# Recurrent stage of a fused attention and mixture kernel: decay spread two units ahead, gather two units behind, three buffers

## The reference, cut to what matters

```
q, k, v = x @ Wq, x @ Wk, x @ Wv                     # x normalised; 16 heads of 8
gk = log_sigmoid(x @ Wg1 @ Wg2 + bg2) / 16
S_t = exp(gk_t)[..., None] * S_{t-1} + k_t[..., None] * v_t[..., None, :]   # 8x8 state per head
o_t = einsum('bhdv,bhd->bhv', S_t, q_t) * 8**-0.5
o = o * rsqrt(mean(o * o) + 1e-5) * g_norm_w
out = (o * silu(x @ Wg)) @ Wo
```

## Time and profile before

| what | value |
|---|---|
| median of three runs | 3115.16 us |
| the runs | 3121.03, 3115.16, 3100.48 us |
| the profiled execution | 3110.69 us |
| its span (first to last instruction) | 3109.0 us |
| mean granted TensorE clock | 0.936 |
| recurrent stage in it | from 2386 us to 2707 us |
| first scan, last scan | 2419.53 us, 2685.09 us |
| first scans of sequences 1, 2 and 3 | 2482.73, 2557.41 and 2633.93 us |

### The profile page before, as it was taken

The page is one execution under the profiler, slowest core; times in us unless marked ns, Lnnn a source line. Parts: engine busy times, 40 slices in busy tenths (PEclk is TensorE's granted clock), DMA queues, the critical chain, the costliest instruction groups (busy, mean ns, idle before and its releaser), DMA issues. The chain is left out here.

```text
span 3109.0 us, 52571 instructions
## 1 busy us (share of the span) xinstructions
PE 2797.3 (90%) x19478; PEld 1590.0 (51%) x19478; DVE 2397.8 (77%) x3680; ACT 2185.3 (70%) x3838; POOL 279.6 (9%) x462
## 2 busy tenths in 40 slices
PE   6869999869999999969999999999998677799999
PEld 4644444423333333344444456778885344478887
DVE  6678999599999999568999364677775666677776
ACT  2358888759999999856888632388886444278887
POOL 1030000200000000030000020100000333210000
PEclk9969999979999999978999789899998888899999
DMA  1043220030000010043211030021111546211111
GB/s 30 0 130 67 43 42 2 23 95 22 22 22 22 22 22 12 1 127 70 43 28 17 2 84 1 1 58 45 46 49 42 156 135 168 69 44 53 55 49 48
DMA packets 96489, 153.02 MB, mean 49 GB/s; under 512 B 16080, under 2 KB 40688, under 8 KB 96240
## 3 DMA queue, kind: packets, MB, share of 16 engines
q1 hardware_dynamic: 96240, 149.74, 19.1%
HBM read 119.29 MB, written 29.62 MB: 48 GB/s over the span
## 5 line engine op out<-in xcount | busy, mean ns | idle before, releaser
L842 DVE TENSOR_REDUCE nested_a_halves<-banks 128x2 f32<-128x1024 f32 x512 | 612.9, 1221 | 62.1 <-PE banks L934 58.7
L889 ACT ACTIVATE nested_a_p<-banks 128x512 f32<-128x512 f32 x1024 | 553.7, 597 | 110.0 <-PE banks L964 84.4
L842 DVE TENSOR_REDUCE wide_a_halves<-banks 128x2 f32<-128x1024 f32 x512 | 593.7, 1217 | 33.5 <-PE banks L934 32.5
L889 ACT ACTIVATE wide_a_p<-banks 128x512 f32<-128x512 f32 x1024 | 554.4, 597 | 45.1 <-PE banks L964 33.9
L1789 DVE TENSOR_TENSOR mix_e_h_low<-mix_e_h,mix_e_h_high 128x512 fp32r<-128x512 f32 x512 | 350.4, 688 | 175.3 <-ACT mix_e_h_high L1918 168.1
L1933 ACT ACTIVATE mix_e_h<-banks,mix_b_folded 128x512 f32<-128x512 f32 x512 | 353.4, 691 | 108.4 <-PE banks L1995 108.2
L977 PE MATMUL banks<-nested_a_p,nested_values 128*32 128x256 f32 x4096 | 328.3, 400 | 0.0
L977 PE MATMUL banks<-wide_a_p,wide_values 128*32 128x256 f32 x4096 | 322.0, 392 | 0.0
L1918 ACT ACTIVATE mix_e_h_high<-mix_e_h 128x512 fp32r<-128x512 f32 x512 | 320.0, 625 | 0.0
L934 PE MATMUL banks<-nested_k_stack,nested_q_stack 48*128 48x512 f32 x1024 | 269.3, 521 | 42.1 <-DMA nested_q_stack<-nested_q_parts 21.8
L964 PE MATMUL banks<-nested_q_stack,nested_k_stack 50*128 50x512 f32 x1024 | 252.6, 423 | 11.2 <-ACT nested_a_p L889 10.3
(11 more groups left out here) (348 smaller groups left out, 3937.6 us busy)
## 6 DMA issues: line engine op xcount, KB each, us to landing
mix_e_gate<-mix_gates_t SPq DMA_DIRECT2D x128, 256.0 KB, 3.2
rec_k_p<-rec_k_rows SPq DMA_DIRECT2D x64, 256.0 KB
rec_v_p<-rec_v_rows SPq DMA_DIRECT2D x128, 128.0 KB
nested_q_stack<-nested_q_parts SPq DMA_DIRECT2D x96, 128.0 KB
nested_q_parts<-nested_q_cut SPq DMA_DIRECT2D x16, 512.0 KB
nested_k_parts<-nested_k_cut SPq DMA_DIRECT2D x16, 512.0 KB
nested_k_stack<-nested_k_parts SPq DMA_DIRECT2D x32, 256.0 KB
mix_raw_w<-L_ffn_w_t SPq DMA_DIRECT2D x16, 512.0 KB, 8.1
```

The costliest lines, as they stand in the source:

```text
L842: dve.tensor_reduce(halves[:, half, i, 2 * a:2 * a + 2], bank[:, at:at + 2, :], AX, ALU.max).then_inc(maxed, 1)
L889: act.activation(p[:, kt % 4, j, :], bank[:, ST + n % RING, :], ACT.Exp, scale=scale).then_inc(probs, 1)
```

## The change

- Decay: PE spreads the decay of unit u + 2 at the head of iteration u, ACT copies it at the head of its iteration u into one of three buffers `decay_p`. The two spreads of decay and q are functions of their own.
- Gather: PE gathers unit u - 2 in iteration u, from one of three buffers `q_state`; all tail steps stand one iteration later (offsets 3, 5, 7, 9 on ACT; 4, 9, 10 on PE; 6, 8, 11 on DVE). The loops run one iteration longer.
- `o_t` and `y` are now one buffer; the copy into it waits for the second transpose of the half before instead of the first.
- First sequence: DVE, not ACT, copies K and V out of PSUM; ACT goes from |z| straight to exp and ln. On DVE `wo_normed` and the 8 copies that make `gather` move behind the gate steps, and both `rest_q` come ahead of gate step 1. PE spreads the first two decays ahead of the two G projections, and ACT copies them ahead of the two silu.
- The semaphore `kept` becomes one each for z, k, v and q.

```diff
-        kv, decay_p, q_state = sb("kv", [P, PRODUCTS, BANK]), sb("decay_p", [P, 2, BANK]), sb("q_state", [P, 2, BANK])
+        kv, decay_p, q_state = (sb(n, [P, PRODUCTS, BANK]) for n in ("kv", "decay_p", "q_state"))
...
+        o_t = y
...
-                    wait_past(dve, gathered, u - 1)
+                    wait_past(dve, gathered, u - PRODUCTS + 1)
...
-                dve.tensor_scalar(wo_normed[:], wo[:], norm[:], None, ALU.mult).then_inc(made, 1)
...
-                dve.wait_ge(made, 3)
+
+                for tile, n in ((k_t, K), (v_t, V)):
+                    for c in range(2):
+                        dve.wait_ge(projected, 2 * n + c + 1)
+                        dve.tensor_copy(tile[:, half(c)], bank[:, FRONT + c, :]).then_inc(kept[n], 1)
+                gate(0, 0)
+                for c in range(2):
+                    rest_q(0, c)
+                gate(0, 1)
+                gate(0, 2)
+                dve.tensor_scalar(wo_normed[:], wo[:], norm[:], None, ALU.mult).then_inc(made, 1)
+                dve.wait_ge(made, 2)
                 for s in range(PAIRS):
                     dve.tensor_copy(gather[:, s, 2 * DH * s:2 * DH * (s + 1)], same[:]).then_inc(made, 1)
...
-                    for offset, part in ((5, 0), (7, 1), (10, 2)):
+                    for offset, part in ((6, 0), (8, 1), (11, 2)):
...
-                        wait_past(act, turned, n)
+                        wait_past(act, y_turned, n)
...
+                def copy_decay(u):
+
+                    act.wait_ge(decay_spread, u + 1)
+                    wait_past(act, scanned, u - PRODUCTS + 1)
+                    act.activation(decay_p[:, u % PRODUCTS, :], bank[:, DECAY, :], ACT.Copy).then_inc(decay_copied, 1)
...
                 for part in range(3):
                     gate(0, part)
-                    if part == 0:
-                        for n in range(2, 6):
-                            keep(0, n)
...
+                copy_decay(0)
+                copy_decay(1)
                 for n in range(8, 10):
                     keep(0, n)
-                for u in range(ALL + 11):
+                for u in range(ALL + 12):
                     b, i = u // UNITS + 1, u % UNITS
-                    if u < ALL:
-                        act.wait_ge(decay_spread, u + 1)
-                        wait_past(act, scanned, u - 1)
-                        act.activation(decay_p[:, u % 2, :], bank[:, DECAY, :], ACT.Copy).then_inc(decay_copied, 1)
-                    for offset, part in ((2, 0), (4, 1), (6, 2), (8, 3)):
+                    if u + 2 < ALL:
+                        copy_decay(u + 2)
+                    for offset, part in ((3, 0), (5, 1), (7, 2), (9, 3)):
...
-                for n in range(10):
+                for n in range(8):
                     project(0, n)
-                pe.wait_ge(made, 3 + PAIRS)
-                spread(0)
-                for u in range(ALL + 11):
+                pe.wait_ge(made, 1)
+                spread_decay(0)
+                spread_decay(1)
+                spread_q(0)
+                for n in range(8, 10):
+                    project(0, n)
+                for u in range(ALL + 12):
                     b, i = u // UNITS + 1, u % UNITS
+                    if u + 2 < ALL:
+                        spread_decay(u + 2)
                     if u + 1 < ALL:
-                        spread(u + 1)
-                    if 1 <= u <= ALL:
-                        gather_unit(u - 1)
-                    for offset, part in ((3, 0), (8, 1), (9, 2)):
+                        spread_q(u + 1)
+                    if u == 2:
+                        pe.wait_ge(made, 3 + PAIRS)
+                    if 2 <= u <= ALL + 1:
+                        gather_unit(u - 2)
+                    for offset, part in ((4, 0), (9, 1), (10, 2)):
```

More of the change, by code:

```diff
@@ L2063, in recurrent_stage @@
     w_in, filled, made, folded, fold_copied = s_("w_in"), s_("filled"), s_("made"), s_("folded"), s_("fold_copied")
-    projected, kept, q_rest, silu_ready = s_("projected"), s_("kept"), s_("q_rest"), s_("silu_ready")
+    projected, q_rest, silu_ready = s_("projected"), s_("q_rest"), s_("silu_ready")
+    kept = [s_(f"{n}_kept") for n in "zkvq"]
     gate_steps, gate_min, gates_out, decay_cut, decay_rest = (
@@ L2109, in store @@
                     for tile, dram, n in ((k_t, k_dram, K), (v_t, v_dram, V)):
-                        sp.wait_ge(kept, b * 8 + 2 * n + 2)
+                        sp.wait_ge(kept[n], b * 2 + 2)
                         wait_past(sp, outer, (b - 1) * UNITS)
@@ L2172, in gate @@
                     if part == 0:
-                        dve.wait_ge(kept, b * 8 + 2)
+                        dve.wait_ge(kept[Z], b * 2 + 2)
                         wait_past(dve, gates_out, b)
@@ L2186, in rest_q @@
                 def rest_q(b, c):
-                    dve.wait_ge(kept, b * 8 + 2 * Q + c + 1)
+                    dve.wait_ge(kept[Q], b * 2 + c + 1)
                     wait_past(dve, q_spread, (b - 1) * UNITS)
@@ L2236, in scan @@
                         start = state[:, 0, s, BANK - 1:BANK]
-                    dve.tensor_tensor_scan(state[:, c, s, :], decay_p[:, u % 2, :], kv[:, u % PRODUCTS, :], start,
+                    dve.tensor_tensor_scan(state[:, c, s, :], decay_p[:, u % PRODUCTS, :], kv[:, u % PRODUCTS, :], start,
                                            ALU.mult, ALU.add).then_inc(scanned, 1)
@@ L2319, in gate @@
                     if part == 0:
-                        act.wait_ge(kept, b * 8 + 2)
+                        act.wait_ge(kept[Z], b * 2 + 2)
                         act.activation(size[:], z_t[:], ACT.Abs).then_inc(gate_steps, 1)
@@ L2409, in project @@
                     else:
-                        pe.wait_ge(kept, b * 8 + n - 1)
+                        pe.wait_ge(kept[kind - 1], b * 2 + c + 1)
                     if kind == G:
@@ L2428, in spread, with spread_q @@
                     for part in range(2):
-                        last = pe.matmul(bank[:, DECAY, :], pick[:, cols], decay_parts[part][:, b % 2, half(c)],
+                        last = pe.matmul(bank[:, DECAY, :], pick[:, s * P:(s + 1) * P], decay_parts[part][:, b % 2, half(c)],
                                          start=part == 0, stop=part == 1)
                     last.then_inc(decay_spread, 1)
+                def spread_q(u):
+                    b, c, s = u // UNITS, u % UNITS // PAIRS, u % PAIRS
+                    if u % UNITS == 0:
+                        pe.wait_ge(q_rest, b * 2 + 2)
                     wait_past(pe, read, u - 1)
                     for part in range(2):
-                        last = pe.matmul(bank[:, QUERY + u % 2, :], pick[:, cols], q_parts[part][:, b % 2, half(c)],
+                        last = pe.matmul(bank[:, QUERY + u % 2, :], pick[:, s * P:(s + 1) * P], q_parts[part][:, b % 2, half(c)],
                                          start=part == 0, stop=part == 1)
@@ L2443, in gather_unit @@
                         wait_past(pe, got, n - 1)
-                    pe.matmul(bank[:, GATHERED + n % 2, :], gather[:, s, :], q_state[:, u % 2, :], start=(s == 0),
+                    pe.matmul(bank[:, GATHERED + n % 2, :], gather[:, s, :], q_state[:, u % PRODUCTS, :], start=(s == 0),
                               stop=(s == PAIRS - 1)).then_inc(gathered, 1)
```

21 lines of the change are left out of this document (7 added, 14 removed).

## The result

The changed kernel took 3089.53 us (median of 20 runs, 3077.48 to 3104.34), the kernel before 3116.32 us in 20 runs beside it (3100.48 to 3132.84). The ratio is 0.9916 with a 95% interval of 0.990 to 0.9933: 0.84% faster. That lies in the predicted range (3042 to 3094), 23 us above the forecast of 3066, outside the band of 3050 to 3075 that had a chance of 0.50, and inside the 1% that the prediction called no change, to which it gave 0.18.

What follows compares the result with a forecast made beforehand. In the recurrent stage no engine is full; a chain of waits, mostly scans waiting for the copied decay, sets the time. 60.1 + 6.2 + 2.6 + 1.9 - 10 - 12 - 3 = 45.8 us off 3110.7, forecast 3066, range 3042 to 3094.

Steps and rivals of the forecast that it cites:

- rival A: DVE's scans against POOL's products: all 64 scans are caught, -37 us in place of -10, so 3093 us; chance 0.13.
- the decay two ahead: In the loop, scans' waits for ACT's copied decay go when it stands two places earlier: +60.1 us.
- DVE's tails: Waits of the additions to x in the loop shrink from 8.7 to about 2.5 us: +6.2 us.
- the start: Ahead of the loop, the first scan starts at 2416.9 instead of 2419.53: +2.6 us.
- the end: Behind the last scan, read(63) and its gather come first and the transposes follow the normalising: +1.9 us.
- the lock: SBUF port shared by DVE and POOL: products hold up 29 scans by 0.79 us each, 10 us more than now: -10.
- V's trip: V's copy, store and spread through memory stall scan 14, and gate step 1 waits for ACT's ln: -12 us (4 to 20).
- PE's order: PE's in-order queue has less cover, waiting at i = 14 for the decay's low part: -3 us (0 to 8).
- B: Decay copy gains only one unit of slack; longer waits leave 17 us in all: 3083 us; chance 0.14.
- C: DMA engines are the bound, at 161 GB/s; sequences 1 and 2 take 65 us: 3077 us; chance 0.13.
- E: ACT's decay copy still arrives late because q's wait for a read holds PE: 3107 us; chance 0.04.

Runs made afterwards that it cites:

- f: Changed kernel with the decay spread one unit ahead and copied in its own iteration again, as before; 3112.16 us, ratio 1.0001.
- g: Changed kernel with the order ahead of the loop as before the change, decay still two ahead; 3098.03 us, one run.
- d: Changed kernel with POOL multiplying only columns 0 to 255 of each product, a measure only; 3071.71 us, ratio 0.9851.
- c: Changed kernel with V's spreads in sequences 1 to 3 reading sequence 0's rows without waiting, a measure only; 3080.56 us, ratio 0.9892.
- a: Changed kernel with ACT's root of a tail moved ahead of the decay copy; 3078.43 us, ratio 0.9882.
- e: Changed kernel with the gather one unit behind and every tail step an iteration sooner, as before; 3075.85 us, ratio 0.9871.
- k: Changed kernel with the gather one behind, tails an iteration sooner, and ACT's root ahead of the decay copy; 3076.93 us, ratio 0.9875.
- b: Changed kernel with DVE's moments of the next sequence moved ahead of the tail steps in iteration 0; 3074.29 us, ratio 0.9862.
- l: Changed kernel with ACT's root ahead of decay copy, DVE's moments ahead of tail, ACT's ln behind V's second copy, POOL's product halved; 3055.98 us, ratio 0.9808.

## Why the prediction was right on the main mechanism and forecast twice the gain

The decay's distance did what was forecast. The measured time lies in the range only because the range's high end was rival A's 3094, and A's reason is not what happened; that much is luck. Point by point, in us of the stage, forecast and found in the change (the found column adds up DVE's waits and stretches):

| term | forecast | found | from |
|---|---|---|---|
| the decay two ahead | +60.1 | +59.8 | waits for the copy 0.3 in all; f brings them back |
| DVE's tails | +6.2 | +1.1 | x additions in the loop 8.7 to 7.6 |
| the start | +2.6 | +3.2 | first scan; g |
| the end | +1.9 | +0.9 | last scan to last addition |
| the lock | -10 | -9.1 | scans 6.5, normalising 2.6; d |
| V's trip | -12 | -19.2 | scan 14: 4.29, 4.08 and 3.59, c; gate step 1: 7.2, which c leaves |
| PE's order | -3 | -13.5 | the root's wait, 13.8 less 0.3; a, e, k |
| not in the sum | 0 | -1.0 | two waits of 0.5 for a product |
| sum | 45.8 | 22.2 | measured: 21.8 |

**The step that failed** is "PE's order": it listed what queues behind PE at i = 14 as "q(31), a gather and the last G projection; none is due within the next scan", and put 3 us on it, 8 at most. Two things were missing. The next sequence's *second decay*, decay(33) there, decay(17) at the turn shown, now queues in that place as well; that it is early for its scan was true, and is why no scan waited. And I followed PE's queue but not ACT's behind it: ACT takes the copy of that decay ahead of the tail's root, and the tail stands on DVE ahead of everything. The delay came out one engine further, at an instruction of another unit. a shows that the order of two statements on ACT carried it; e and k show that the gather's distance had brought the root into that place.

**V's trip** was the right mechanism for scan 14, with a size at the end of its range (4 to 20). The stall there was 3.6 to 4.3 us where I had 3, and in all three sequences, where I had 2 us in all for sequence 0; from store to product it took 6.3 to 7.0 us, close to the 6.3 forecast. The other part, gate step 1, waited 1.8 to 3.1, and c shows that the trip does not set it. I allowed V's copy to come 47 us into a sequence; it came at 54.8, since ACT itself ran late by the stall at the turn: in a and b, which shorten that stall, it comes at 48.2 and 46.9. Scan 14 still waits 3.9 and 3.5 us in those.

**The lock** came out near its size only with a part that was not forecast: the scans cost 6.5 us more, where I had 10, and normalising 2.6.

**DVE's tails**: half right. The waits of the additions at the first two turns went, as argued: 2.58 and 1.85 us before, none after; that of the third stayed (1.72 and 1.71). But in the middle of sequences 1 and 2 they grew from 0.85 and 0 to 1.88 and 2.64, which I had not walked. In the loop they are 8.7 us before, 9.7 in e, 6.8 in f, 7.6 in the change: the gather's distance spares 2 us, not 6.

**The rivals.** A (all scans caught) gave 3093 and the kernel took 3089.5, but not for A's reason: the excess is 19.6 us, not 50.6. B is refuted, as none of its 17 us of left-over waits is there. C is refuted by the rates: its bound of 161 GB/s was exceeded in the change (169 and 172), and l moved 193 in sequence 1. E is refuted, as the waits for the decay copy are gone. That a program with hand-written orders has further places where one engine's queue holds up another's, up to 4 us at a turn, had no share in my chances and should have had.

## What to carry to other kernels

When a step is moved earlier in in-order queues, follow its own inputs at the boundary where they come late, and list what stands behind it on *each* engine that now waits for it, not only who waits for its result: work made two units ahead is early everywhere but at the turn, and there it holds up the urgent work behind it. Put the step with the nearer due time first (here two swapped statements took 18 us off a stage of 298), and move a distance only where a trace shows a wait for it: one distance here gave 35 us (with the new start), the other took 13 back. Savings found one at a time overlap: a and b took 18 and 17 us of stage, but 20 together.

## What the runs showed of the hardware that was not expected

The normalising step was stretched by the products as the scans were. Eight `tensor_scalar` with one large SBUF input took 2.14 us in sequences 1 and 2 before and 3.45 in both after, each time with a product inside (here from 2493.09 to 2494.38):

```profile
2491.77 3.45 DVE L2170 TENSOR_SCALAR rec_h<-x_resident,rec_ln_moments,rec_ln_rstd 128x128 f32<-128x128 f32 x8
2493.09 1.29 POOL L2155 TENSOR_TENSOR rec_kv<-rec_k_p,rec_v_p 128x512 f32<-128x512 f32 x1 [0.76 <-DMA rec_v_p<-rec_v_rows]
```

The difference, 1.31 us, is the product's length; in d, with products of half the columns, the same step took 2.67 and 2.65. The Trainium skill ("SBUF — State Buffer", section "Who interferes with whom") says that `tensor_scalar` can enter a mode in which it takes the ports it shares with GpSimd too; the trace agrees. The prediction took DVE's other work as free of the lock; this step is not.

Behind PE's idle stretch at the turn its granted clock fell to half (the windows view of the changed kernel, columns as in the earlier trace rows):

```profile
2464.40:2469.50 5.10, 0.02 (x1) 0.00 (x0) 4.00 (x6) 0.35 (x1) 2.29 (x2) 0.94 0.71 164
2469.50:2475.60 6.10, 6.07 (x16) 4.55 (x17) 4.15 (x5) 2.48 (x3) 2.20 (x1) 0.50 0.75 211
```

PE did 0.02 us of work in 5.10 us, and then 6.07 of 6.10 us at 0.50, which is 1.2 GHz. At the third turn (2610 to 2616 us) it was 0.53. A gather took 1.91 us there and 1.02 behind it. So the wait for the low part of the decay cost PE twice, and the spread of decay(17), for which ACT and the root waited, stood in just that stretch. How much of the 13.5 us is the clock and how much the wait was not separated.
